# Graph attention and edge convolution on one Trainium2 core: the second share of a turn's gather products, issued without the wait for the first share's completion

## What is computed

```
h = relu(layernorm(x))
for l in (1, 2, 3):                       # attention layers, 4 heads of 16
    xl, xr = h @ Wl, h @ Wr
    s      = leaky_relu(xl[src] + xr[dst])
    e      = sum(s * a) per head
    alpha  = softmax of e over the edges of one dst
    h      = segment_sum(xl[src] * alpha, dst) + b     # relu between layers
x = x + h
h = relu(layernorm(x))
agg = segment_sum(relu(h[src] + edge_attr @ W_edge.T + b_edge), dst)
x = x + MLP with batch norm over the nodes (h + agg)
```

## Time and profile before

| | us |
|---|---|
| median of three runs | 8745.62 |
| lowest and highest run | 8744.52, 8752.81 |
| profiled execution, first to last instruction (its span) | 6476.7 |
| median less span | 2268.9 |
| PE busy with matmuls | 5692.6 (88% of the span) |
| DVE busy | 4958.1 (77%) |
| ACT busy | 4658.0 (72%) |
| POOL busy | 4758.4 (73%) |

### The profile page before, as it was taken

One profiled execution on the slowest core, in us unless ns is written; L12 is line 12 of the kernel. 1 busy time (PEld: TensorE's weight loads), 2 busy tenths in 40 slices (PEclk: granted clock), 3 DMA queues, 4 the chain that ended last, 5 costly groups with the idle time before them and its releaser, 6 DMA issues.

```text
span 6476.7 us, 96630 instructions
## 1 busy us (share of the span) xinstructions
PE 5692.6 (88%) x25094; PEld 4699.3 (73%) x25094; DVE 4958.1 (77%) x7554; ACT 4658.0 (72%) x6121; POOL 4758.4 (73%) x4960
## 2 busy tenths in 40 slices
PE   2699999999679999999949999999968999999996
PEld 1577787777468888888738888888846777777774
DVE  8699999999669999999939999999984344334433
ACT  1588888888468888888828888888854555555553
POOL 3777777777677777777777777777767777777774
PEclk9899999999789999999959999999978999999996
DMA  9577777777345555555525555555544444444441
GB/s 390 193 243 240 240 239 240 241 240 243 117 136 177 181 179 174 178 182 176 172 73 174 177 174 180 182 174 175 181 122 112 142 141 142 136 143 139 144 141 52
DMA packets 453281, 1147.44 MB, mean 177 GB/s; under 512 B 159661, under 2 KB 224799, under 8 KB 417669
## 3 DMA queue, kind: packets, MB, share of 16 engines
q1 hardware_dynamic: 279472, 919.26, 39.5%
q0 software_dynamic: 159376, 175.97, 15.2%
q10 hardware_dynamic: 14404, 51.92, 2.0%
HBM read 750.45 MB, written 396.27 MB: 177 GB/s over the span
## 4 chain that ended last, share of the span: by engine, by line
POOL 38%; issue 25%; DVE 19%; ACT 13%; PE 1%; DMA 1%; ACTq 1%; DVEq 1%; POOLq 0%; SPq 0%
POOL sb_xl L516 33%; DVE pG L1158 6%; DVE sb_s_run L1200 5%; ACT sb_turn_out L719 5%; ACT sb_hot L719 4%; ACT sb_v_in L719 3%; POOL sb_hot_f L516 3%; POOL marks L520 2%; DVE sb_s L1441 2%; ACT pB L719 1%; DVE sb_e_in L1223 1%; DVE sb_lr L1221 1%; DVE sb_s L1219 1%; DVE sb_mark L1104 1%; PE pG L604 1%
## 5 line engine op out<-in xcount | busy, mean ns | idle before, releaser
L604 PE MATMUL pG<-sb_xl_parts,sb_hot 128*128 128x476 f32 (+1 forms) x24010 | 5312.2, 379 | 424.4 <-ACT sb_xl L719 312.0
L604 PEld LDWEIGHTS pG<-sb_xl_parts,sb_hot 128*128 128x128 f32 x24010 | 4486.7, 189 | 1292.4 <-issue 695.9
L516 POOL DMA_INDIRECT sb_xl<-xl_table,sb_idx x4557 | 4363.5, 958 | 1400.6 <-issue 1391.2
L1158 DVE COPY_PREDICATED pG<-sb_pick_turn,pG 128x408 f32<-128x408 int32 (+7 forms) x2352 | 1071.7, 457 | 940.0 <-ACT sb_pick_turn L719 808.0
L719 ACT ACTIVATE sb_hot<-sb_wide 128x1792 fp32r<-128x1792 bf16 (+1 forms) x784 | 1427.5, 1834 | 103.9 <-ACT sb_turn_out L719 67.7
L1200 DVE TENSOR_TENSOR_SCAN sb_s_run<-pB,sb_v_in 128x272 f32<-128x272 f32 (+3 forms) x1470 | 1094.9, 772 | 4.1 <-ACT sb_turn_out L719 4.0
L719 ACT ACTIVATE sb_turn_out<-sb_s_run 128x1088 f32<-128x1088 f32 (+3 forms) x395 | 834.7, 2113 | 11.4 <-DVE sb_s_run L1200 11.1
L719 ACT ACTIVATE sb_xl<-pG 128x136 f32<-128x136 f32 (+4 forms) x826 | 248.1, 303 | 612.9 <-DVE pG L1158 506.0
L1197 DVE TENSOR_TENSOR_SCAN pB<-sb_same_c,pB 128x1024 f32<-128x1024 f32 x294 | 671.7, 2285 | 0.1
L719 ACT ACTIVATE pB<-sb_mark 128x960 f32<-128x960 f32 x294 | 563.8, 1918 | 80.2 <-DMA sb_mark<-marks 62.5
L719 ACT ACTIVATE sb_v_in<-sb_v_g 128x1024 f32<-128x1024 f32 x291 | 601.1, 2065 | 0.0
(11 more groups left out here) (237 smaller groups left out, 2357.2 us busy)
## 6 DMA issues: line engine op xcount, KB each, us to landing
state_rows<-sb_turn_out SPq DMA_DIRECT2D x294, 576.0 KB, 3.4
sb_wide<-hots SPq DMA_DIRECT2D x147, 1120.0 KB
sb_mark<-marks SPq DMA_DIRECT2D x294, 512.0 KB
sb_wide<-hots SPq DMA_DIRECT2D x147, 896.0 KB
sb_xl<-xl_table,sb_idx POOLq DMA_INDIRECT x4557
sb_wide<-codes SPq DMA_DIRECT2D x49, 1120.0 KB
hots<-sb_wide SPq DMA_DIRECT2D x49, 1120.0 KB
marks<-sb_hot_f SPq DMA_DIRECT2D x32, 1568.0 KB
```

The source lines that it names most:

```text
L516: return pool.indirect_dma_start(out=dst, out_offset=None, in_=table, in_offset=bass.IndirectOffsetOnAxis(ap=index, axis=0))
L604: product = pe.matmul(pG[:, bank + a - lo, 0:GB * n], hot[k][:, m, a * P:(a + 1) * P], rows[:, :, 0:n], start=(m == 0 and part == 0), stop ...
L1158: return dve.copy_predicated(rows[:, :, 0:n], over(pick_turn[:, k, stage, lo:hi], n), rows[:, :, at:at + n])
```

## The change

One wait of PE and the increment that follows it are removed. Before, PE held back the first product of share 1 until the last product of share 0 of the same turn had completed and signalled. Now the first product of share 1 waits for its one-hot and for its banks to be free alone. The signals themselves (`s_pg[0]`, `s_pg[1]`), the order of the products and everything on other engines are as before.

```
--- before.py
+++ after.py
@@ -593,9 +593,6 @@
 
                 pe.wait_ge(s_rows[q], copied)
                 pe.sem_inc(s_passed, 1)
-                if q:
-                    pe.wait_ge(s_pg[q - 1], copied + 1)
-                    pe.sem_inc(s_passed, 1)
                 lo, hi, bank = share(k, q, n)
                 for a in range(lo, hi):
                     for m in range(GB):
```

## The result

| comparison | before, us | changed, us | ratio, 95% interval |
|---|---|---|---|
| first | 8745.07 | 8986.01 | 1.0235 [1.0196, 1.0273] |
| repeated, chip 2 | 8745.80 | 8973.27 | 1.0252 [1.0229, 1.0274] |
| repeated, chip 3 | 8741.31 | 8977.59 | 1.0283 [1.0258, 1.0307] |
| repeated, chip 5 | 6475.90 | 6478.71 | 1.0005 [0.9994, 1.0015] |

The times are medians of all runs; the recorded ratio is not exactly their quotient, and in the first comparison it leaves out the changed kernel's longest run (9019.98 us). The prediction was 8745 us, no change. The changed kernel is slower by 2.4% (1.0235), 241 us by the medians. The first interval reaches from 2.0 to 2.7%; the two repeats on chips 2 and 3 lie clear above 2%.

The account below looks back on a forecast made before the run. POOL's gather steps were taken as the bound, in layer 1 with DVE. Loops gain 0, exposed ends 0.35 to 0.7 us: span 6476.7 to about 6476.1 us, plus 2268.9 us outside, gives 8745 us; range 8736 to 8755 us.

Parts of the forecast that it names:

- the sum: Whole kernel: span 6476.7 us goes to about 6476.1; with 2268.9 us outside it unchanged, 8745 us.
- What bounds the kernel: All passes: POOL's gather steps, 1.250 us each in layer 2, are the limit, in layer 1 together with DVE.
- The bubble: PE's pause between share 0 and share 1: 0.35 us at each of 392 boundaries, 137 us of PE time, hidden in the loops.
- DVE's wait at the end of layer 1: DVE waiting there for PE's share 1: 0.61 us, to shrink to about 0.3 us.
- The wait that was to take up the bubble: PE's wait for ACT's copy ahead of share 0: 0.3 to 0.4 us longer, linear stage 113.8 to about 145 us.
- What is late next: After the change nothing new is last: POOL's gather steps stay the last, in layer 1 with DVE.
- no wait is added: Cost of the change: none seen, so the gain could not fall below nothing; cost bounds 0 to 2 us.
- The rivals: Three alternatives: PE is the bound, 5%; the clock falls in the linear stage, 3%; the bubble stays despite the change, 5%.
- The clock's fall: Linear stage: longer PE idle lowers the granted clock, 2.0 us per turn, 196 us more, 8942 us; chance 3%.
- PE as the bound: PE limits layers 2 and 3: 69 us less, 8677 us; with all 392 turns 137 us less, 8608 us; chance 5%.
- The chance of slower: Whole kernel slower by over 0.2%: 4%, of which 3% for the clock and 1% unseen.

Follow-up runs that it names:

- another variant: Kernel before with one wait more: share 0 also waits for the previous turn's share 1; 6481.12 us on chip 6, one of ten executions 8240.01 us.

## Why the prediction was wrong

**The step that failed** is in the sum: "Against the median of 8745.62 us, of which 2268.9 us lie outside the span and which I take to stay as they are ..." Nothing lies outside but 1.8 us. A difference of 35% between the metric and the only profile was taken as an offset, while it said that the timed executions had 2249 us of waits that the profile did not. Every later sentence was about another regime than the one that was timed.

**What bounds the kernel.** "So POOL never stops for another engine in that pass": right on the fast chips, by the run with fewer products (479.8 us for 392 gathers). Wrong on chip 3: POOL stops for DVE for 2225 us, and DVE for PE's signals.

**The bubble.** 0.35 us a boundary, hidden in the loops: it measured 0.30 us, and it is hidden on the fast chips, where the whole change is +2.8 us by the medians, inside the interval around none. The forecast there was 0.6 us less. Not all marks came as forecast: DVE's wait at the end of layer 1 is 0.91 us in place of 0.61, where 0.3 was forecast. The wait that was to take up the bubble did grow. In the linear stage PE's wait for ACT's copy rose from 113.8 us to this, on chip 5, the forecast being about 145:

```profile
PE pG L601 <- ACT sb_xl L716: 155.4, 94, 3.9
```

**What is late next: "Nothing new".** On a slow chip a new thing is late: share completions, recorded some 20 us after their products in the longest cases. There the removed wait was not a bubble but a stop of 1714.9 us in total.

**"Below nothing I see no price here: no wait is added."** There was one, +372 us, less the 133 of the linear stage. The traces show where: share 1's signals, late in 3 of 294 attention turns with the wait, are late in 122 without it. My reading is that PE, once it no longer stops at share 0's late signal, goes on and puts share 1's products behind it, so that their signal is late as well; no run varied this alone.

**The rivals.** None was the case. The clock's fall, at 3%, was nearest in sign and size (8942 us), by a mechanism that the runs do not support: on a slow chip the mean clock of a pass is 0.83 to 0.89 with the wait and 0.84 to 0.86 without it, and it falls behind PE's stops. On the fast chip 5 the change did lower the mean grant, from 0.959 to 0.955, while the time rose by no more than the 3 us above. PE as the bound is refuted on a fast chip by the run with fewer products. The chance of slower, 4%, and the range of 8736 to 8755 us had no case in which the trace at hand was not a trace of the timed runs.

**What stays open.** Why completions come late on chips 2 and 3, and whether it is the chip or something else that held for those comparisons. The matmul ends in a trace are modelled, so the rows don't tell whether the products themselves or only their signals are late. SP shows that more than PE is held: of 1266 DMA issues of four lines in the loops 332 take over 0.6 us in the kernel before on chip 3 and 415 in the changed one, where in the first profile 44 do. The same DMA issue on the changed kernel's trace, inside the stall above and behind it:

```profile
3400.53 0.70 SPq L374 DMA_DIRECT2D sb_mark<-marks  x1
...
3428.17 0.33 SPq L374 DMA_DIRECT2D sb_mark<-marks  x1
```

The Trainium skill, NOTIFIC — the notification-queue block, section 7.1 Overflow: three behaviours, one of which stalls the engine, says that inside the block that writes trace records a full pipeline holds back the engines that produce records. That would fit stalls on PE and SP and the single products 2 to 3 us apart. The recording does differ between the kinds of chip: of the 784 signals of the shares, 114 have no record in the kernel before's trace from chip 3 and 55 in the changed kernel's, and in the first profile none is missing. But no run here shows the cause: each execution whose span is known was recorded, on both kinds of chip. By such a cause the 2.4% would be a property of the recorded execution, and it would be gone with the recording.

## What to carry to other kernels

Before the profile is used, put its span beside the timed runs. If they differ by more than a few microseconds, the profile is of another regime: the difference is the first thing to explain, and a forecast needs a case for each regime. A wait that an engine makes on its own work may be free where signals are prompt and decide where they are late. Here it helped where the consumer takes the parts one by one and hurt where it needs both of them; but one more wait helped in the second place too, so this is what one kernel did and not a rule. And where a profile misses records, add up all the idle time ahead of an instruction before you compare one class of waits.

## What the runs showed of the hardware

Two times, for one program and one input: medians of 6476 to 6485 us on chips 4, 5, 6, 8 and 12, and of 8737 to 8746 us on chips 2 and 3. The kernel before is steady within 0.3% in each comparison; the changed kernel scatters by up to 0.5% on chips 2 and 3. One execution of another variant on chip 6 took 8240.01 us. In the changed kernel on chip 3 share 0's completion signal lands a median of 3.0 us and up to 16.9 us after the recorded end of its last product, and share 1's 19.4 us or more in a tenth of the turns; in the first profile and on chip 5 every one lands within 0.02 us. In the stretches before a late signal SP's DMA issues take about 0.70 us each in place of 0.33 us. A PE wait on its own last product costs 0.30 us where signals are prompt (0.52 in place of 0.22 us from start to start). A gather takes the same on both kinds of chip: a median of 0.944 us in the changed kernel on chip 3, 0.945 us in the earlier trace rows.
